# Scores whose products also deliver k transposed, in an attention and routed-weights kernel

## The reference

```python
q = gelu(xn @ W1q + b1q) @ W2q + b2q        # k and v likewise; xn = layernorm(x)
scores = (q @ k.T) / sqrt(256 * 512) * tril  # causal, no softmax
x = x + layernorm(scores @ v) * ln_w + ln_b
idx = argmax(pe @ sign(tile_sigs).T)         # one of 8 weight tiles for each position
x = x + (layernorm(x) @ W[idx].T + b[idx])
```

## Time and profile before

| | value |
|---|---|
| median of three runs | 310.03 us |
| span of the profiled execution, first to last instruction | 307.9 us |
| mean granted clock of TensorE | 0.989 |
| TensorE busy, products | 289.4 us, 94% |
| TensorE busy, weight loads | 259.1 us, 84% |
| VectorE busy | 231.8 us, 75% |
| ScalarE busy | 198.4 us, 64% |
| GpSimd busy | 163.3 us, 53% |

### The profile page before, as it was taken

The page is one execution under the profiler, slowest core; times in us unless marked ns, Lnnn a source line. Parts: engine busy times, 40 slices in busy tenths (PEclk is TensorE's granted clock), DMA queues, the critical chain, the costliest instruction groups (busy, mean ns, idle before and its releaser), DMA issues.

```text
span 307.9 us, 5596 instructions
## 1 busy us (share of the span) xinstructions
PE 289.4 (94%) x1874; PEld 259.1 (84%) x1874; DVE 231.8 (75%) x514; ACT 198.4 (64%) x391; POOL 163.3 (53%) x229
## 2 busy tenths in 40 slices
PE   6899999999999999999999999999999898889990
PEld 6778989898789889888978898889898898889970
DVE  4697779789977966986697579758956888767661
ACT  2388567767586778578667865886877554688000
POOL 3710622190479174927544653557364575777771
PEclk9989999999999999999999999999999999999997
DMA  8819961001110211111131100027021361393220
GB/s 203 285 43 245 362 206 34 0 2 68 34 57 18 90 51 38 42 60 38 36 104 36 56 18 0 2 73 200 2 92 36 88 198 55 126 333 119 80 68 18
DMA packets 24193, 27.84 MB, mean 90 GB/s; under 512 B 4643, under 2 KB 22052, under 8 KB 24102
## 3 DMA queue, kind: packets, MB, share of 16 engines
q1 hardware_dynamic: 15750, 13.29, 14.6%
q0 software_dynamic: 3296, 8.64, 8.1%
q10 hardware_dynamic: 5120, 5.55, 5.6%
HBM read 13.95 MB, written 14.44 MB: 92 GB/s over the span
## 4 chain that ended last, share of the span: by engine, by line
PE 59%; DVE 18%; issue 5%; DMA 5%; ACT 5%; POOL 4%; SPq 1%; POOLq 0%; DVEq 0%; ACTq 0%
PE ring L463 33%; PE o_ps L463 9%; PE s_ps L463 5%; PE sc_ps L463 5%; POOL out_dram L1688 3%; DMA w_stage<-w1v 3%; DVE xres L1179 2%; PE ring L476 2%; PE w_ps L463 1%; PE ring L557 1%; DMA slot_rows<-sorted_rows 1%; DVE xnT L1098 1%; DMA sorted_rows<-xres,slot_i 1%; DVE st L1186 1%; DVE hT L1103 1%
## 5 line engine op out<-in xcount | busy, mean ns | idle before, releaser
L463 PE MATMUL ring<-xnT,w_sp 128*128 128x512 f32 x288 | 75.0, 406 | 2.1 <-issue 1.0
L463 PEld LDWEIGHTS ring<-xnT,w_sp 128*128 128x128 f32 x288 | 53.1, 193 | 14.8 <-DVE hT L1103 1.9
L836 ACT ACTIVATE ring<-ring,b_cols 128x512 f32<-128x512 f32 x48 | 31.7, 660 | 24.5 <-PE ring L463 23.4
L463 PE MATMUL ring<-hT,w_sp 128*128 128x512 f32 x192 | 46.4, 397 | 0.0
L1103 DVE TENSOR_TENSOR hT<-ring,hT 128x512 fp32r<-128x512 f32 x48 | 32.6, 684 | 13.9 <-ACT hT L839 13.3
L463 PEld LDWEIGHTS ring<-hT,w_sp 128*128 128x128 f32 x192 | 35.4, 188 | 8.1 <-DVE hT L1103 0.2
L1643 POOL DMA_INDIRECT sorted_rows<-xres,slot_i x30 | 30.7, 1023 | 8.4 <-issue 6.6
L1609 POOL TENSOR_TENSOR vtok<-v,vtok 128x512 fp32r<-128x512 f32 x14 | 17.7, 1282 | 30.7 <-ACT vtok L858 30.7
L1590 POOL TENSOR_SCALAR nm<-mv 128x4 f32<-128x4 f32 x8 | 1.8, 229 | 57.5 <-DVE mv L1085 57.5
L839 ACT CAST hT<-ring 128x512 fp32r<-128x512 f32 x48 | 28.2, 587 | 1.5
L463 PE MATMUL o_ps<-state,qT 128*128 128x256 f32 x174 | 26.6, 290 | 0.0
(11 more groups left out here) (210 smaller groups left out, 614.2 us busy)
## 6 DMA issues: line engine op xcount, KB each, us to landing
sorted_rows<-blank ACTq DMA_DIRECT2D x1, 5032.0 KB, 18.1
xt<-x SPq DMA_DIRECT2D x8, 512.0 KB, 3.5
slot_rows<-sorted_rows SPq DMA_DIRECT2D x22, 136.0 KB, 3.0
w_stage<-tile_w SPq DMA_DIRECT2D x8, 256.0 KB, 2.8
h<-sorted_rows SPq DMA_DIRECT2D x15, 136.0 KB, 3.6
hT<-position_table POOLq DMA_DIRECT2D x1, 512.0 KB, 6.5
sorted_rows<-xres,slot_i POOLq DMA_INDIRECT x30, 2.6
row_stage<-rows ACTq DMA_DIRECT2D x1, 384.0 KB, 7.7
```

The lines of the kernel that those rows point to most:

```text
L463: last = te.matmul(o, lhs[k][a], rhs[k][c], start=start and k == 0 and i == 0, stop=stop and k == n - 1 and i == 2, skip_group_check=check)
L836: nc.scalar.activation(full, ring[(2 + m) % 3][:, :], ACT.Gelu, bias=b1c[:, m // 2, m % 2:m % 2 + 1]).then_inc(gelu, 1)
```

## The change

An identity is stored beside the high part of every 128 columns of q (q_eye: q's high part, then the identity). In a chunk's scores, the products that had q's high part as moving operand, kT high by q high and kT low by q high, now run over 256 columns. Their first half is the score as before. Their second half is kT turned by the identity, high plus low, that is k with tokens on partitions. The product with q's low part (q_low) stays 128 wide. A chunk so fills 384 columns of a bank (scores, then k's two halves; for the second half of the channels the output is in two pieces), and the chunks go to four places, `kept`: sc_ps, w_ps, ring[2] and sc_ps again, so that chunk 3 waits until chunk 0 has been read and masked. k32, its copy and the eight transposes are gone. The masked scores go to sc32 in SBUF, from which both parts of scT are made.

TensorE, start of the kernel, before: v, the transposes of k32, the scores and the next xn.

The core of the diff:

```diff
-FILLS = 16
+FILLS = 14
...
-        k32 = sb("k32", [P, KC, GT])
-        qT = sb("qT", [P, 2, KC, GT], F32R)
+        q_eye = sb("q_eye", [P, KC, CH, 2, P], F32R)
+        q_low = sb("q_low", [P, KC, CH, P], F32R)
...
+        kept = [sc_ps, w_ps, ring[2], sc_ps]
...
             def front_transposes(s, first):
                 te.wait_ge(xn_done, s + 1)
+                if not first:
+                    te.wait_ge(v_sum, 2 * s)
                 for k in range(KC):
-                    if not first:
-                        te.wait_ge(v_sum if k else ktok_lo, 2 * s)
...
+                    elif m == 0 and s:
+                        te.wait_ge(sc_mask, CH * s - 1)
...
             def front_scores(s):
                 te.wait_ge(q_lo, 2 * s + 2)
                 te.wait_ge(k_lo, 2 * s + 2)
-                if s:
-                    te.wait_ge(sc_lo, s)
+                if s == 0:
+                    te.wait_ge(eye_set, 1)
+                else:
+                    te.wait_ge(wf_lo, tiles_turned(s))
                 for c in range(CH):
-                    last = mm3(sc_ps[:, cols(c)], [[kT[:, a, k, cols(c)] for a in range(2)] for k in range(KC)],
-                               [[qT[:, a, k, cols(c)] for a in range(2)] for k in range(KC)])
-                last.then_inc(scores, 1)
-            def front_ktok(s):
-                for n in range(2):
-                    if n == 0:
-                        te.wait_ge(k_lo, 2 * s + 2)
-                    else:
-                        te.wait_ge(v_sum, 2 * s + 1)
-                    for i in range(4):
-                        last = te.transpose(ring[(14 + n) % 3][:, cols(i)], k32[:, i % 2, cols(2 * n + i // 2)],
-                                            ident[:, :])
-                    last.then_inc(fill, 1)
+                    if c == CH - 1:
+                        te.wait_ge(sc_mask, CH * s + 1)
+                    o = kept[c][:, 0:P]
+                    both = kept[c][:, :].rearrange("p (a n) -> p a n", a=2)
+                    for k in range(KC):
+                        wide = both[:, :, 0:P] if k else kept[c][:, 0:2 * P].rearrange("p (a n) -> p a n", a=2)
+                        k_hi_c, k_lo_c = [kT[:, a, k, cols(c)] for a in range(2)]
+                        te.matmul(wide, k_hi_c, q_eye[:, k, c], start=k == 0, stop=False, skip_group_check=True)
+                        te.matmul(o, k_hi_c, q_low[:, k, c, :], start=False, stop=False, skip_group_check=True)
+                        last = te.matmul(wide, k_lo_c, q_eye[:, k, c], start=False, stop=k == KC - 1,
+                                         skip_group_check=True)
+                    last.then_inc(scores, 1)
...
                 if c == 0:
                     te.wait_ge(v_lo, 2 * s + 2)
-                    te.wait_ge(ktok_lo, 2 * s + 2)
...
+                    te.wait_ge(ktok_lo, CH * s + c + 1)
...
-            def k_rounded(s):
-                for j in range(2):
-                    act.wait_ge(fill, FILLS * s + 11 + j)
-                    nc.scalar.activation(k32[:, j, :], ring[(10 + j) % 3][:, :], ACT.Identity,
-                                         bias=b2c[:, K, j:j + 1]).then_inc(k_full, 1)
-                    act.wait_ge(k_full, 2 * s + 1 + j)
-                    nc.scalar.copy(kT[:, 0, j, :], k32[:, j, :]).then_inc(k_hi, 1)
+            def k_rounded(s, j):
+                act.wait_ge(fill, FILLS * s + 11 + j)
+                nc.scalar.activation(kT[:, 0, j, :], ring[(10 + j) % 3][:, :], ACT.Identity,
+                                     bias=b2c[:, K, j:j + 1]).then_inc(k_hi, 1)
...
                 if s < LAST:
-                    act.wait_ge(sc_mask, s + 1)
+                    act.wait_ge(sc_mask, CH * s + CH)
                 else:
                     act.wait_ge(diagonal, CH - 1)
-                full = sc32 if s == LAST else sc_ps
-                nc.scalar.copy(scT[:, 0, :], full[:, :]).then_inc(sc_hi, 1)
-            def ktok_rounded(s):
-                for n in range(2):
-                    act.wait_ge(fill, FILLS * s + 15 + n)
-                    nc.scalar.copy(ktok[:, 0, 2 * n:2 * n + 2, :],
-                                   ring[(14 + n) % 3][:, :].rearrange("p (c d) -> p c d", c=2)
-                                   ).then_inc(ktok_hi, 1)
+                nc.scalar.copy(scT[:, 0, :], sc32[:, :]).then_inc(sc_hi, 1)
+            def ktok_rounded(s, c):
+                act.wait_ge(scores, CH * s + c + 1)
+                nc.scalar.copy(ktok[:, 0, c, :], kept[c][:, P:P + C]).then_inc(ktok_hi, 1)
...
                 lead_norm(s + 2, (1,))
-                k_rounded(s + 1)
+                k_rounded(s + 1, 0)
                 lead_norm(s + 2, (2,))
+                k_rounded(s + 1, 1)
+                lead_norm(s + 2, (3,))
                 v_rounded(s + 1, 0)
-                lead_norm(s + 2, (3,))
+                ktok_rounded(s + 1, 0)
                 v_rounded(s + 1, 1)
-                ktok_rounded(s + 1)
+                for c in range(1, CH):
+                    ktok_rounded(s + 1, c)
...
+            def chunk_rest(s, c):
+                dve.wait_ge(ktok_hi, CH * s + c + 1)
+                nc.vector.tensor_tensor(ktok[:, 1, c, :], kept[c][:, P:P + C], ktok[:, 0, c, :].bitcast(F32),
+                                        ALU.subtract).then_inc(ktok_lo, 1)
+                nc.vector.tensor_tensor(sc32[:, cols(c)], kept[c][:, 0:P], tril[:, :], ALU.mult).then_inc(sc_mask, 1)
...
             def scores_rest(s):
                 dve.wait_ge(sc_hi, s + 1)
-                full = sc32 if s == LAST else sc_ps
-                nc.vector.tensor_tensor(scT[:, 1, :], full[:, :], scT[:, 0, :].bitcast(F32),
+                nc.vector.tensor_tensor(scT[:, 1, :], sc32[:, :], scT[:, 0, :].bitcast(F32),
                                         ALU.subtract).then_inc(sc_lo, 1)
...
-                q_rest(s + 1)
+                q_rest(s + 1, (0,))
                 state_rest(s, 3)
+                q_rest(s + 1, (1,))
+                x1_final(s, (0,))
                 k_rest(s + 1, 0)
-                x1_final(s, (0,))
+                x1_final(s, (1,))
                 k_rest(s + 1, 1)
                 v_biased(s + 1, 0)
-                x1_final(s, (1,))
+                x1_final(s, (2,))
                 v_biased(s + 1, 1)
-                ktok_rest(s + 1)
-                scores_masked(s + 1)
-                x1_final(s, (2,))
+                for c in range(CH):
+                    chunk_rest(s + 1, c)
                 xnT_rest(s + 2)
                 scores_rest(s + 1)
+                state_rest(s + 1, 0)
                 x1_final(s, (3,))
-                state_rest(s + 1, 0)
...
             pool.wait_ge(small_in, 32)
             residual(0)
+            nc.gpsimd.tensor_copy(q_eye[:, :, :, 1, :].rearrange("p k c n -> p (k c) n"),
+                                  ident[:, :].unsqueeze(1).broadcast_to([P, KC * CH, P])).then_inc(eye_set, 1)
             nc.gpsimd.memset(blank[:, :], 0.0).then_inc(blank_set, 1)
```

More of the change, by code:

```diff
@@ L325, in pair_rows, with q_chunk, q_from @@
             return None
+        kept = [sc_ps, w_ps, ring[2], sc_ps]
+        def q_chunk(k, c):
+            return [q_eye[:, k, c, 0, :], q_low[:, k, c, :]]
+        def q_from(k, j):
+            return [q_eye[:, k, j:CH, 0, :], q_low[:, k, j:CH, :]]
         off_at = [0, 3 * P, 5 * P]
@@ L572, in back_state @@
                     te.wait_ge(s_lo, splits_before(s, c))
-                    mm3(o, [[qT[:, a, k, cols(c)] for a in range(2)] for k in range(KC)],
+                    mm3(o, [q_chunk(k, c) for k in range(KC)],
                         [[state[:, a, k * C:k * C + C] for a in range(2)] for k in range(KC)], stop=False)
@@ L652, in last_scores @@
                     te.wait_ge(v_sum, 2 * STEPS - 1)
-                last = mm3(sc_bank[j], [[kT[:, a, k, cols(j)] for a in range(2)] for k in range(KC)],
-                           [[qT[:, a, k, j * P:GT] for a in range(2)] for k in range(KC)])
+                last = mm3(sc_bank[j].rearrange("p (c n) -> p c n", n=P),
+                           [[kT[:, a, k, cols(j)] for a in range(2)] for k in range(KC)],
+                           [q_from(k, j) for k in range(KC)])
                 if j != 2:
@@ L666, in last_state @@
                     te.wait_ge(o_cen, i - 2)
-                mm3(last_o[c][:, 0:C], [[qT[:, a, k, cols(c)] for a in range(2)] for k in range(KC)],
+                mm3(last_o[c][:, 0:C], [q_chunk(k, c) for k in range(KC)],
                     [[state[:, a, k * C:k * C + C] for a in range(2)] for k in range(KC)], stop=False)
@@ L1048, in _ @@
             slot_norm(6)
-            k_rounded(LAST)
+            k_rounded(LAST, 0)
+            k_rounded(LAST, 1)
             slot_rounded(5)
@@ L1117, in k_rest @@
                                                op0=ALU.add, op1=ALU.subtract).then_inc(k_lo, 1)
-            def ktok_rest(s):
-                for n in range(2):
```

(9 more changed lines are left out.)

31 lines of the change are left out of this document (15 added, 16 removed).

## The result

The changed kernel takes 304.88 us, the median of four runs (304.78 to 304.93), against 309.94 (309.77 to 310.3) for the kernel before on the same chip: a ratio of 0.9831, 95% interval 0.9817 to 0.9845. It is 5.1 us faster. The forecast was 312.7, slower; what came is the first rival, VectorE first in all seven steps, for which the working had 304.7.

The account below looks back on a forecast made before the run. TensorE's issue and waits through the attention steps were taken to bound the kernel. Span 307.9, +1.8 for lost and won races, +0.9 for the identity's copy gave 310.6; with 2.1 around the span, 312.7 us, range 303.6 to 313.8.

Parts of the forecast that it names:

- the first rival: VectorE's scT subtraction starts before GpSimd's residual addition in all seven attention steps: 304.7 us, chance 0.28.
- The walk to the race: Start times worked out within a step: VectorE's scT subtraction at 5.25 to 5.28, GpSimd's residual addition at 5.30.
- T0: Zero of a step's times: v's products all issued; k's transposes begin before the change, the first score product after.
- its wait: TensorE's chunk 3 waits until chunk 0's bank is read and masked: 0 to 0.03 a step.
- the scT subtraction: VectorE's subtraction for scT's rest, now with both inputs in SBUF; if the residual began first, ends 0.55 after it.
- the residual: GpSimd's residual addition in each step, expected at T0 + 5.30 and taking 2.41.
- a lead of 0.03 loses and one of 0.12 wins, and I take it that the residual wins in steps 1, 3, 4, 5 and 6: Race for SBUF between VectorE and GpSimd: the residual first in five steps, 312.7 us, chance 0.52.
- The row at 124.83: VectorE addition in the earlier trace, read as starting 0.03 before GpSimd's tile operation yet being held, 0.77 for 0.47.
- The price of a lost race: With the residual first, TensorE's scT products start at T0 + 8.41 where before it was 7.47: +0.94.
- The identity's copy, +0.9: GpSimd's 128x1024 copy at the kernel's start holds VectorE's weight subtractions: +0.9.
- Step 1: Attention step where VectorE's routing work already held TensorE for 0.42; the first rival gains about 0.4 there.
- The reordering priced at nothing: VectorE's reordered additions and state subtraction find their inputs ready: 0; without that cover 0.4 a piece.

Follow-up runs that it names:

- e11: Changed kernel with the last addition to xres put back in front of the state's rest; 307.53 us, ratio 0.9921 to the kernel before.
- e9: Changed kernel with a 128x384 ScalarE copy in front of the scores' rounding in steps 1 to 6; 315.27 us, ratio 1.0215 to the kernel before.
- e7: Changed kernel with a 192-column VectorE memset in front of the scT subtraction in steps 1 to 6; 320.82 us, ratio 0.9905 to the kernel before.
- e8: Changed kernel with ScalarE rounding v's second half before the key copy of chunk 0; 329.54 us, ratio 1.0199 to the kernel before.
- e10: Changed kernel with TensorE making the eight transposes of the next xn twice in steps 1 to 6; 318.24 us, ratio 1.0258 to the kernel before.
- e3: Changed kernel with the identity's copy moved behind rstd_lead(1) on GpSimd; 316.6 us, ratio 0.9826 to the kernel before.
- e1: Changed kernel with one one-column VectorE memset in front of the scT subtraction in steps 1 to 6; 317.49 us, ratio 0.9859 to the kernel before.
- e2: Changed kernel with three one-column VectorE memsets in front of the scT subtraction in steps 1 to 6; 317.21 us, ratio 0.9854 to the kernel before.
- e4: Changed kernel with GpSimd's residual addition moved behind rstd_lead, later in the step; 320.77 us, ratio 0.9955 to the kernel before.
- e12: Changed kernel with the identity's copy moved behind rstd_lead(1) on GpSimd, run again in another set; 304.31 us, ratio 0.9828 to the kernel before.

## Why the prediction was wrong

**The walk to the race was right.** Transposes of xn at T0 + 2.80 (predicted 2.77), chunk 3's first product at 2.10 (2.08, so its wait costs 0.02 at most), the scT subtraction at 5.25 to 5.26 (5.25 to 5.28), the residual at 5.31 to 5.34 (5.30). Steps 0 and 2 fell as it had them.

**The step that failed is "a lead of 0.03 loses and one of 0.12 wins, and I take it that the residual wins in steps 1, 3, 4, 5 and 6".** The lead was 0.05 to 0.08, where the walk had 0.02 to 0.05, since the residual came up to 0.04 later than counted; and VectorE won in all five steps (the subtraction 0.68), as it did with 0.046 in e11. So the edge that I read from one row of another pair of operations was not this pair's: it lies below a lead of 0.05. With nothing ahead of it for 0.13, a start 0.13 behind the residual lost (e9); directly behind a memset, a start 0.13 to 0.16 behind did not (e7); directly behind an xnT subtraction, 0.24 behind lost (e8). Where between 0.05 ahead and 0.13 behind the edge lies was not run without a memset.

The row at 124.83 was not a race that a lead of 0.03 decides. The addition and GpSimd's second tile operation start within 0.03 of each other in five steps of the kernel before, the addition ahead in two and behind in three. It takes 0.72 to 0.77 in all five and ends 0.74 to 0.75 after the tile operation's start, whoever was first. Here the addition is 0.03 behind (the tile operations of the second line start at 64.76 and 65.69):

```profile
65.72 0.72 DVE L1179 SCALAR_TENSOR_TENSOR xres<-cen,rs,xres 128x256 f32<-128x256 f32 x1
```

```profile
64.76 1.87 POOL L1677 TENSOR_SCALAR w_stage<-w_stage 128x255 f32<-128x255 f32 x2
```

Why that hold lasts only 0.3 stays open; no run here was made on it. The 0.52 for the forecast against 0.28 for the rival rested on this row alone.

**The Trainium skill** (SBUF — State Buffer, SBUF: two separate sides) says that whoever of the two starts first has the shared ports for the whole instruction. By that rule the walk, 5.25 against 5.30, gave the race to VectorE, and I set it behind one row that seemed to contradict it. The runs agree with it in the changed kernel (0.05 to 0.08 ahead, 0.68), in e8, e9 and e10 (behind, and held past the residual's end); e7's subtraction, 0.13 behind and not held, does not fit it.

**The price of a lost race was nearly right where it was worked out and missed a part behind it.** Predicted: scT products at T0 + 8.41, 0.94 later than before. Measured in e9: 8.30, 0.83 later, but the steps are 1.3 longer than before, with the second gap. The forecast for that case, 312.7, has beside it e9's 313.92 in the profiled execution and 315.27 in the median of three.

**The identity's copy, +0.9,** was the right size within a set: 0.86 between e3 and the mean of e1, e2 and e4 of its set (33.41 less 32.55). In the profiled execution after, the start is 1.10 later by another sum. The landing of w1v took 8.8 us for 7.8, so VectorE's first pair of weight subtractions started at 13.53 for 12.53, 1.0 later. That was past the residual's hold, which had cost 0.5 (1.79 for the pair before, where e12's, held by nothing, takes 1.28), but the copy held the pair for 0.6 (1.89). So that the rival's 304.7 stands so near 304.88 is in part luck: 1.10 for its 0.9 was made of other terms, and the median is 1.8 above the span, not 2.1.

**Step 1.** The rival had a gain of 0.4 there, and 0.33 came. The rival's sum for the steps was -6.2, measured -5.98.

**The reordering priced at nothing** cost nothing, as said, but I did not ask what it was worth: 2.7 us (e11), because the operation that the residual holds is now one that nobody needs soon. The addition behind the subtraction is held whenever the subtraction wins; e11 is what that costs with the state behind it.

## What to carry to other kernels

When two engines meet on a shared resource, who is first is worth more than what either does: here a start 0.2 us later on one engine cost 9.1 us (e9). Find the pair of starts, work out both to a few hundredths, and if they are that close, give both outcomes an equal chance, whatever a single row of another pair suggests. Recorded starts that differ by 0.02 do not tell who was first. Then look at what stands behind the loser, and put there the operation that is needed last.

## What the runs showed of the hardware

- VectorE's 128x512 subtraction, 0.13 behind the residual's start, took 0.63 directly behind a memset (e7) and 2.78 after an idle 0.13 (e9). Directly behind an xnT subtraction, 0.24 and 0.58 behind the residual, it was held (2.68 in e8, 2.37 in e10).
- The loser's end follows the winner's: 0.28 after the residual for the 128x256 addition, 0.55 for the 128x512 subtraction. A residual that VectorE holds takes 2.85 for 2.41 and ends 2.24 to 2.27 after the subtraction, as if it did nearly all of its work behind it.
- A held operation of 32 columns took 2.37 (e4): the hold does not depend on how little the loser has to do.
- Products of 256 columns cost TensorE hardly more than those of 128: 18 products, 12 of them wide, in 2.10 us, 0.117 each, for 0.113 in the earlier trace rows.
